# The third projection in lent score banks, value work of the first unit on GpSimd, and the choice of experts spread over the first steps

## The chip, the cores and the metric

One Trainium2 chip, one core of it. The time is that of the whole program on the device in microseconds, the median of several executions. TensorE (PE) multiplies, VectorE (DVE), ScalarE (ACT) and GpSimd (POOL) do the rest, each in the order of its own queue; semaphores tie them together. SyncE issues the DMAs.

## The reference, cut to what matters

Eight stages work one after the other on a residual of 2 sequences of 1024 tokens with 128 channels. The last and the last but two are the same stage with the same weights, and the change touches that one alone. It is attention with experts: 8 heads, 5 experts a head of which the best 3 count by a gate, 64 channels a head.

```python
ss = jax.nn.sigmoid(x @ Ws).reshape(b, t, H, E)
sd = jax.nn.sigmoid(x @ Wd).reshape(b, t, H, E)
ms, md = _topk_mask(ss, K), _topk_mask(sd, K)
q = jnp.einsum('bthed,bthe->bhtd', q5, sd * md)
k = jnp.einsum('bthed,bthe->bhtd', k5, ss * ms)
v = jnp.einsum('bthed,bthe->bhtd', v5, ss * ms)
attn = jax.nn.softmax(jnp.einsum('bhid,bhjd->bhij', q * scale, k), axis=-1)
out = jnp.einsum('bhij,bhjd->bihd', attn, v)
```

q5, k5 and v5 are the token times a weight of 5 x 64 columns for each head. The output of a head is sent through a second weight for each chosen expert and summed.

## The kernel before, in words

`expert_attention_stage` (from L2166) runs twice. A unit is a pair of heads of one sequence: 8 units of 8 tiles of 128 tokens, 64 tiles in all. A tile needs three projections (kinds 0 query, 1 key, 2 value), each for two heads: `project` (L2303) writes 320 columns into each of two PSUM banks, and DVE's `apply_gates` (L2607 for queries, L2610 for keys and values) multiplies both by the gates into `scratch`, the product; each kind has two buffers there. POOL's `sum_queries` (L2505 to L2507, three additions) and DVE's `sum_keys` (L2624) and `sum_values` (L2617) add the five experts.

Ahead of the steps the queries and keys of the first 8 tiles are made, then the 8 tiles of values, then queries and keys of 3 tiles more. Then 64 steps run, one a tile of queries. In step j PE makes the scores of j + 1 (L1504, two heads in banks 0 to 3), turns two blocks of the exponentials (L1515, bank 4), multiplies the values of step j - 1 (L1545, bank 5, 24 matmuls a head), and subtracts (L1524). Beside this it makes three projections, `beside(0)` to `beside(2)`: the value tile j + 8, the query and the key tile j + 11, each pair of heads in banks 6 and 7 (`spare`), each waiting until `product_ready` tells that the pair ahead is read. `first(j)` is the number of the step's first projection. From step 53 on only values are left, from 56 on nothing. In steps with t = j mod 8 of 2 and 6 `turn` (L2309) transposes four tiles of queries and of keys of the next unit, into banks 0 and 1, and ACT's `place` (L2430) copies them out.

DVE takes in step j: the maximum of the scores of head 0 (L1594), product, maximum of head 1, product, sum of values, reciprocal and routing of step j - 1 (`route`, L1601 and L1606), product, sum of keys. ACT takes: copy of the turned blocks (`act_copy`, L1571), exponential of head 0 (L1558), its high part in bf16 (`act_hi`, L1565), exponential of head 1, the rest (`act_rest`, L1575), high part of head 1. POOL takes: the low parts of step j (`pool_lo`, L1581, 768 and 1024 columns), counts, the sum of queries, and the sum of the routed output of j - 1 into z (L2493, from unit 2 on two sums, L2495 and L2496). SyncE sends high and low parts through the transposing DMA to PE's value matmuls.

At t = 0 and 4 half a unit's values are split in bf16: ACT makes the high half (`act_split_values`, L1619), POOL the low one (`pool_split_values`, L1623); for the first unit DVE does the latter (`dve_split_values`, L1628).

The choice of experts for a pair of heads: `compare` on DVE (four compares with `ahead` as output, L2587), 8 `count_duels` on POOL (L2516, L2518), `limit` on DVE (L2593), `keep` on POOL (L2525), and `chosen` lets DVE begin the queries of that pair.

Of the kernel before, what the change touches and what calls it, by code (L numbers as in the profile page):

```python
# [2165 lines left out]
def expert_attention_stage(core, tag):  # L2166
# [10 lines left out]
    with ExitStack() as ctx:  # L2177
# [29 lines left out]
        v_ready = sem("v_ready")  # L2207
# [24 lines left out]
        def last_of(tile, kind):  # L2232
# [5 lines left out]
            return 6 * T + 4 * (tile - T) + 2 * kind + 1 if tile < LEAD else first(tile - LEAD) + 2 * kind + 3  # L2238

# [34 lines left out]
        def _(pe):  # L2274
# [74 lines left out]
            for j in range(STEPS):  # L2349
                unit, t = j // T, j % T  # L2350
                turning = t in (2, 6) and unit + 1 < UNITS

                def beside(k):
                    n = first(j) + 2 * k
                    if n < first(j + 1):
                        pe.wait_ge(product_ready, n // 2)
                        for h in range(2):
                            project(n + h, spare[h])

                finishing = done_in(t) if unit + 1 == UNITS else ()  # L2360

                if j == STEPS - T:
                    pe.wait_ge(product_ready, first(STEPS) // 2)
                if j + 1 < STEPS:
                    if t in (3, 7) and unit + 1 < UNITS:
                        pe.wait_ge(qk_ready, (unit + 1) * 4 + t // 4 * 2 + 2)
                    hs.scores(pe, j + 1)
                beside(0)
# [7 lines left out]
                beside(1)  # L2376
                hs.subtract(pe, j)
                if turning:
                    pe.wait_ge(hs.exp_done, 2 * j + 3)
                    for i in range(2):  # L2380
                        turn(unit + 1, t // 4 * 2 + i, core.ps[i])
                if j:
                    hs.values(pe, j - 1, 1)
                beside(2)
# [13 lines left out]
        def _(act):  # L2398
# [48 lines left out]
            for i in range(2):  # L2447
                hs.act_split_values(act, 0, i, (v_ready, T // 2 * (i + 1)))
            for j in range(STEPS):
# [937 lines left out]
```

## Time and profile before

| | |
|---|---|
| median of 3 runs (lowest to highest) | 2641.14 us (2640.59 to 2646.53) |
| profiled execution: time, span | 2640.06 us, 2638.3 us |
| busy PE, PE weight load | 2353.3 us (89%), 1517.7 us (58%) |
| busy DVE, ACT, POOL | 2009.1 us (76%), 1480.1 us (56%), 1804.6 us (68%) |
| mean granted TensorE clock | 0.953 of full speed |
| L2303, projections of both stages | 508.7 us busy |
| L1581, low parts on POOL | 478.5 us busy |

The span is the time from the first instruction to the last on the core. Busy shares are over the whole span, so they average eight stages; what one step costs is read from the timelines of one step. In a timeline "x4" are four records of one group; a matmul in f32 leaves two records, so a projection of both heads is x4 and a set of scores x8. A tag in brackets gives the idle time before an instruction and what ended it.

### The profile page before, as it was taken

The page shows a single profiled execution, that of the slowest core. Times are in us where ns is not written, and L with a number is a line of the kernel's source. Part 1 is how long each engine was busy: PE and PEld are TensorE (multiplying, and loading weights), DVE is VectorE, ACT ScalarE, POOL GpSimd, SP SyncE. Part 2 cuts the span into 40 slices and gives each one's busy share as a digit, 9 for nine tenths or more (in the row PEclk, how much of TensorE's full clock was granted, in tenths as well). Part 3 has the DMA queues.
Part 4 walks back from the last instruction along what each step waited for, and adds up shares of the span by engine and source line. Part 5 has one row for each costly group of instructions (what it writes and reads, how often), then busy time and mean ns, then how long its engine had stood idle before and what let it go on. Part 6 is the DMA issues. An engine that isn't in the chain of part 4 may idle for free. (4 is left out here: it accounts for less than half of the span.)

```text
span 2638.3 us, 55375 instructions
## 1 busy us (share of the span) xinstructions
PE 2353.3 (89%) x21054; PEld 1517.7 (58%) x21054; DVE 2009.1 (76%) x3656; ACT 1480.1 (56%) x2085; POOL 1804.6 (68%) x1704
## 2 busy tenths in 40 slices
PE   6788777888799999999978999999879799999987
PEld 3555534644466667666655666666533556666655
DVE  7998555545677777777669999999567899999974
ACT  4222122332688888888834566556744256655665
POOL 0888300000699999999946899999820388999986
PEclk9899779889899999999989999999989899999999
DMA  1000000000698989889943666666710256666666
GB/s 46 1 1 0 1 24 14 1 24 17 134 160 151 163 148 162 159 151 163 145 112 64 113 113 117 119 116 113 140 40 0 70 95 117 113 119 116 117 113 122
DMA packets 829353, 243.48 MB, mean 92 GB/s; under 512 B 811528, under 2 KB 820232, under 8 KB 829088
## 3 DMA queue, kind: packets, MB, share of 16 engines
q1 hardware_dynamic: 829088, 239.93, 49.6%
q8 instruction: 168, 2.75, 0.4%
q14 instruction: 97, 0.79, 0.1%
HBM read 20.70 MB, written 1.05 MB: 8 GB/s over the span
## 5 line engine op out<-in xcount | busy, mean ns | idle before, releaser
L2303 PE MATMUL banks<-g_w,normed_t 128*128 128x320 f32 x1536 | 508.7, 457 | 23.9 <-DVE g_scratch L2610 11.0
L1581 POOL TENSOR_TENSOR g_p_lo<-g_p,g_p_hi 128x768 bf16<-128x768 f32 (+1 forms) x256 | 478.5, 1891 | 35.7 <-POOL g_z L2496 23.2
L1786 DVE TENSOR_REDUCE at_negmax<-banks 128x1 f32<-128x1024 f32 x256 | 301.4, 1219 | 154.6 <-PE banks L1698 154.6
L2303 PEld LDWEIGHTS banks<-g_w,normed_t 128*128 128x128 f32 x1536 | 262.3, 189 | 209.9 <-DVE g_scratch L2610 85.8
L1763 POOL TENSOR_TENSOR at_p_lo<-at_p,at_p_hi 128x640 bf16<-128x640 f32 x256 | 356.9, 1415 | 12.9 <-ACT at_p_hi L1751 11.3
L1594 DVE TENSOR_REDUCE g_negmax<-banks 128x1 f32<-128x1024 f32 x256 | 310.3, 1217 | 42.0 <-PE banks L1504 42.0
L1744 ACT ACTIVATE at_p<-banks,at_negmax 128x1024 f32<-128x1024 f32 x256 | 285.7, 1116 | 6.2 <-DVE at_negmax L1786 6.2
L1558 ACT ACTIVATE g_p<-banks,g_negmax 128x1024 f32<-128x1024 f32 x256 | 285.2, 1114 | 5.6 <-DVE g_negmax L1594 5.3
L1698 PE MATMUL banks<-at_k_t,at_q 64*128 64x512 f32 x1024 | 258.0, 622 | 18.2 <-POOL at_k_t L2047 9.5
L1504 PE MATMUL banks<-g_k_t,g_q 64*128 64x512 f32 x1024 | 254.4, 615 | 12.6 <-ACT g_p L1558 7.2
L1571 ACT CAST g_r_hi<-banks 128x256 bf16<-128x256 f32 x128 | 47.7, 372 | 380.8 <-PE banks L1515 380.8
L1565 ACT CAST g_p_hi<-g_p 128x768 bf16<-128x768 f32 (+1 forms) x256 | 241.7, 944 | 5.6 <-DMA g_t_lo<-g_p_lo 1.6
L1545 PE MATMUL banks<-g_v_hi,g_t_hi 128*128 128x65 bf16 x1792 | 191.5, 194 | 26.9 <-DMA g_t_lo<-g_p_lo 26.5
L2610 DVE TENSOR_TENSOR g_scratch<-banks,g_gate 128x640 f32<-128x640 f32 x256 | 209.7, 820 | 6.8 <-PE banks L2303 1.4
L1545 PEld LDWEIGHTS banks<-g_v_hi,g_t_hi 128*128 128x128 bf16 x1792 | 165.6, 98 | 51.4 <-DMA g_t_lo<-g_p_lo 37.1
L1545 PE MATMUL banks<-g_v_lo,g_t_hi 128*128 128x65 bf16 x1792 | 191.4, 194 | 0.0
L1770 POOL TENSOR_TENSOR at_u_lo<-at_u 128x768 bf16<-128x768 f32 x128 | 189.0, 1477 | 3.2 <-ACT at_u L1757 2.6
L1545 PE MATMUL banks<-g_v_hi,g_t_lo 128*128 128x65 bf16 x1792 | 190.3, 194 | 0.0
L1751 ACT CAST at_p_hi<-at_p 128x640 bf16<-128x640 f32 x256 | 185.9, 726 | 7.7
L1545 PEld LDWEIGHTS banks<-g_v_lo,g_t_hi 128*128 128x128 bf16 x1792 | 165.8, 98 | 2.4
L1545 PEld LDWEIGHTS banks<-g_v_hi,g_t_lo 128*128 128x128 bf16 x1792 | 166.0, 98 | 0.0
L1504 PEld LDWEIGHTS banks<-g_k_t,g_q 64*128 64x128 f32 x1024 | 88.3, 186 | 123.7 <-issue 96.2
(419 smaller groups left out, 5995.8 us busy)
## 6 DMA issues: line engine op xcount, KB each, us to landing
at_swapped<-at_crossed SPq DMA_DIRECT2D x128, 128.0 KB, 2.8
g_w<-in_ex_w SPq DMA_DIRECT2D x2, 2880.0 KB, 11.5
f_w<-in_W SPq DMA_DIRECT2D x2, 1024.0 KB, 5.5
at_rope<-in_rope SPq DMA_DIRECT2D x1, 2048.0 KB, 9.4
at_t_hi<-at_p_hi SPq DMA_TRANSPOSE x128, 3.7
at_t_lo<-at_p_lo SPq DMA_TRANSPOSE x128, 3.6
g_t_hi<-g_p_hi SPq DMA_TRANSPOSE x128, 4.3
g_t_lo<-g_p_lo SPq DMA_TRANSPOSE x128, 4.2
```

The lines of the kernel that those rows point to most:

```text
L1504: ins = self.nc.tensor.matmul(self.core.ps[2 * h + half], self.q[rows, b, t * P:(t + 1) * P], self.kt[rows, b, half * CHUNK:(half + 1) * C ...
L1545: ins = self.nc.tensor.matmul(self.sums[:, at:at + 65], p, v[:, b, k, h, :], start=(k == 0 and i == 0), stop=(k == self.T - 1 and i == 2))
L1558: self.nc.scalar.activation(self.p[:, j % 2, h, :], self.core.banks[:, 2 * h:2 * h + 2, :], ACT.Exp, bias=self.negmax[:, h:h + 1]).then_in ...
L1565: self.nc.scalar.copy(self.part(self.p_hi, j, h), self.p[:, j % 2, h, 0:self.WIDTH[h]]).then_inc(self.hi_ready, 1)
L1581: self.nc.gpsimd.tensor_tensor(self.part(self.p_lo, j, h), self.p[:, j % 2, h, 0:self.WIDTH[h]], self.part(self.p_hi, j, h), ALU.subtract) ...
L1594: self.nc.vector.tensor_reduce(self.negmax[:, h:h + 1], self.core.banks[:, 2 * h:2 * h + 2, :], AX.XY, ALU.max, negate=True).then_inc(self ...
L1698: ins = self.nc.tensor.matmul(self.core.ps[self.pair(j, h) + half], self.q[rows, b, t * P:(t + 1) * P], self.kt[rows, b, half * CHUNK:(hal ...
L1744: self.nc.scalar.activation(self.p[:, j % 2, h, :], self.core.banks[:, first:first + 2, :], ACT.Exp, bias=self.negmax[:, j % 2, h:h + 1]). ...
L1763: self.nc.gpsimd.tensor_tensor(self.p_lo[:, j % self.RING, h, :], self.p[:, j % 2, h, 0:self.BY_DMA * P], self.p_hi[:, j % self.RING, h, : ...
L1786: self.nc.vector.tensor_reduce(self.negmax[:, j % 2, h:h + 1], self.core.banks[:, first:first + 2, :], AX.XY, ALU.max, negate=True).then_i ...
L2303: nc.tensor.matmul(out[:, 0:ED], core.xt[:, at:at + P], w[:, kind * H + tile // (T * BATCH) * 2 + h, :], start=True, stop=True).then_inc(p ...
L2610: v.tensor_tensor((k_product if kind == 1 else v_product)[:, tile % 2], src.rearrange("p h (c e) -> p h c e", e=E), own.unsqueeze(2).to_br ...
```

## The change

- PE: in a step the first projection (values, still in banks 6 and 7) stands ahead of the scores, the second (queries, banks 6 and 7) behind them, the third (keys) goes to banks 0 and 1 and waits for head 0's exponential. The next scores wait for its product. `turn` uses banks 6 and 7 and waits for the second product. The subtraction stands at the end of the step, but in the last unit.
- DVE: product, sum of values, maximum, product, maximum, then the split of half the values at t = 0 and 4, routing, product, sum of keys. In steps 0 to 7 one compare (`duel`) follows for pairs 2 and 3; `limit` follows in steps 1, 13 and 22, not in 7 and 16.
- ACT: the copy of the turned blocks and `place` stand behind the exponential of head 0, the high half of the values behind the exponential of head 1.
- POOL: no splits in the steps; counts of pairs 2 and 3 in steps 5 to 12 and 14 to 21, `keep` in 3, 15 and 24.
- Ahead of the steps: POOL sums the values of tiles 1, 3, 5 and 7 (`sum_odd_values`) and splits the first unit; DVE compares pairs 0 and 1 alone; POOL counts pair 1 behind the queries of tile 9.

```diff
+
+        def own_sums(tiles):
+
+            return tiles - min(tiles, T) // 2
...
+                pairs = (first(j + 1) - first(j)) // 2
                 finishing = done_in(t) if unit + 1 == UNITS else ()
+
+                def both_heads(k, banks):
+                    for h in range(2):
+                        project(first(j) + 2 * k + h, banks[h])
                 if j == STEPS - T:
                     pe.wait_ge(product_ready, first(STEPS) // 2)
+                if t in (3, 7) and unit + 1 < UNITS:
+                    pe.wait_ge(qk_ready, (unit + 1) * 4 + t // 4 * 2 + 2)
+                if pairs:
+                    pe.wait_ge(product_ready, first(j) // 2 - (1 if j and first(j) - first(j - 1) == 6 else 0))
+                    both_heads(0, spare)
                 if j + 1 < STEPS:
-                    if t in (3, 7) and unit + 1 < UNITS:
-                        pe.wait_ge(qk_ready, (unit + 1) * 4 + t // 4 * 2 + 2)
+                    if pairs:
+                        pe.wait_ge(product_ready, first(j) // 2)
                     hs.scores(pe, j + 1)
-                beside(0)
+                if pairs == 3:
+                    pe.wait_ge(product_ready, first(j) // 2 + 1)
+                    both_heads(1, spare)
                 hs.transpose(pe, j)
...
                 if j:
                     hs.values(pe, j - 1, 0)
-                beside(1)
-                hs.subtract(pe, j)
                 if turning:
-                    pe.wait_ge(hs.exp_done, 2 * j + 3)
+                    pe.wait_ge(product_ready, first(j) // 2 + min(pairs, 2))
                     for i in range(2):
-                        turn(unit + 1, t // 4 * 2 + i, core.ps[i])
+                        turn(unit + 1, t // 4 * 2 + i, spare[i])
+                if unit + 1 == UNITS:
+                    hs.subtract(pe, j)
                 if j:
                     hs.values(pe, j - 1, 1)
-                beside(2)
+                if pairs == 3:
+                    pe.wait_ge(hs.exp_done, 2 * j + 3)
+                    both_heads(2, core.ps[0:2])
+                if unit + 1 < UNITS:
+                    hs.subtract(pe, j)
...
             for i in range(2):
-                hs.act_split_values(act, 0, i, (v_ready, T // 2 * (i + 1)))
+                act.wait_ge(v_odd, T // 4 * (i + 1))
+                hs.act_split_values(act, 0, i, (v_ready, own_sums(T // 2 * (i + 1))))
...
-                hs.act_copy(act, j)
+                if unit + 1 == UNITS:
+                    hs.act_copy(act, j)
                 for k, tile in finishing[0:1]:
                     place_out(k)
                 if not last:
                     hs.act_exp(act, j + 1, 0)
+                if unit + 1 < UNITS:
+                    hs.act_copy(act, j)
+                if t in (2, 6) and unit + 1 < UNITS:
+                    for i in range(2):
+                        place(unit + 1, t // 4 * 2 + i, core.ps[6 + i])
...
-                if t == 0 and unit:
-                    hs.act_split_values(act, unit, 1, (v_ready, (unit + 1) * T))
-                if t == 4 and unit + 1 < UNITS:
-                    hs.act_split_values(act, unit + 1, 0, (v_ready, (unit + 1) * T + T // 2))
                 if not last:
                     hs.act_exp(act, j + 1, 1)
+                if t == 0 and unit:
+                    hs.act_split_values(act, unit, 1, (v_ready, own_sums((unit + 1) * T)))
+                if t == 4 and unit + 1 < UNITS:
+                    hs.act_split_values(act, unit + 1, 0, (v_ready, own_sums((unit + 1) * T + T // 2)))
                 hs.act_rest(act, j)
-                if t in (2, 6) and unit + 1 < UNITS:
-                    for i in range(2):
-                        place(unit + 1, t // 4 * 2 + i, core.ps[i])
...
+            def sum_odd_values(tile):
+                pool.wait_ge(product_ready, (last_of(tile, 2) + 1) // 2)
+                part = v_product[:, tile % 2]
+                step(g.tensor_tensor(part[:, :, :, 0:2], part[:, :, :, 0:2], part[:, :, :, 2:4], ALU.add))
+                step(g.tensor_tensor(part[:, :, :, 0], part[:, :, :, 0], part[:, :, :, 1], ALU.add))
+                g.tensor_tensor(hs.v[:, tile, :, 0:D], part[:, :, :, 0], part[:, :, :, 4], ALU.add).then_inc(v_odd, 1)
+
...
-            for pair in range(2):
-                for k in range(8):
-                    count_duels(pair, k)
-            for pair in range(2):
-                keep(pair)
+            for k in range(8):
+                count_duels(0, k)
+            for tile in (1, 3):
+                sum_odd_values(tile)
+            keep(0)
+            for tile in (5, 7):
+                sum_odd_values(tile)
+            for i in range(2):
+                hs.pool_split_values(pool, 0, i)
             for tile in range(T, LEAD - 1):
                 sum_queries(tile)
+            for k in range(8):
+                count_duels(1, k)
...
-                if j % T == 0 and j:
-                    hs.pool_split_values(pool, j // T, 1)
-                if j % T == 4 and j // T + 1 < UNITS:
-                    hs.pool_split_values(pool, j // T + 1, 0)
-                if j < 18 and j % 9 < 8:
-                    count_duels(2 + j // 9, j % 9)
-                elif j < 18:
-                    keep(2 + j // 9)
+                if 5 <= j < 13:
+                    count_duels(2, j - 5)
+                elif 14 <= j < 22:
+                    count_duels(3, j - 14)
+                if j in (3, 15, 24):
+                    keep(1 + j // 12)
                 if j + LEAD - 1 < TOTAL:
                     sum_queries(j + LEAD - 1)
...
+                if kind == 2 and 2 <= tile < T + 2 and tile % 2:
+                    dve.wait_ge(v_odd, tile // 2)
+                elif kind == 2 and tile >= 2:
+                    dve.wait_ge(v_ready, own_sums(tile - 1))
+                elif tile >= 2:
+                    dve.wait_ge((q_ready, k_ready)[kind], tile - 1)
...
             def sum_values(tile):
+                if tile < T and tile % 2:
+                    return
...
             compare(0)
-            compare(1)
...
-            compare(2)
-            compare(3)
+            compare(1)
...
-                if tile in (4, 6):
-                    limit(tile // 2 - 2)
+                if tile == 4:
+                    limit(0)
...
-                else:
-                    for i in range(2):
-                        hs.dve_split_values(dve, 0, i)
...
-                        apply_gates(n, 6)
+                        apply_gates(n, 0 if k == 2 else 6)
                 finishing = done_in(t) if unit + 1 == UNITS else ()
+                beside(0)
+                if j + T < TOTAL:
+                    sum_values(j + T)
                 if j + 1 < STEPS:
                     hs.dve_max(dve, j + 1, 0)
-                beside(0)
+                beside(1)
                 if j + 1 < STEPS:
                     hs.dve_max(dve, j + 1, 1)
                 if unit + 1 == UNITS and t > 2:
                     add_out(*done_in(t - 1)[1])
-                beside(1)
-                if j + T < TOTAL:
-                    sum_values(j + T)
+                if t == 0 and unit:
+                    hs.dve_split_values(dve, unit, 1)
+                if t == 4 and unit + 1 < UNITS:
+                    hs.dve_split_values(dve, unit + 1, 0)
                 if j:
                     route(j - 1)
                 beside(2)
@@ -2701,8 +2736,12 @@
                     sum_keys(j + LEAD)
                 for k, tile in finishing[0:1]:
                     add_out(k, tile)
-                if j in (7, 16):
-                    limit(2 + j // 9)
+                if j < 2 * (E - 1):
+                    ins = duel(2 + j // (E - 1), j % (E - 1) + 1)
+                    if j % (E - 1) == E - 2:
+                        ins.then_inc(compared, 1)
+                if j in (1, 13, 22):
+                    limit(1 + j // 10)
```

## Rows read from the trace of the kernel before

**Rows 1.** Chain that ended last: start us, us, what; scores of four steps
```profile
2141.84 1.92 PE banks L1504 x8
...
2173.37 1.92 PE banks L1504 x8
...
2301.39 1.92 PE banks L1504 x8
...
2333.23 1.92 PE banks L1504 x8
```

**Rows 2.** Timeline of PE, one plain step: start us, us, engine, line, op, tiles, count
```profile
2206.03 1.99 PE L1504 MATMUL banks<-g_k_t,g_q 64*128 64x512 f32 x8
2207.94 1.34 PE L2303 MATMUL banks<-g_w,normed_t 128*128 128x320 f32 x4
2209.12 0.38 PE L1515 MATMUL banks<-identity,g_p 128*128 128x128 f32 x2
...
2210.20 1.34 PE L2303 MATMUL banks<-g_w,normed_t 128*128 128x320 f32 x4
...
2212.47 1.34 PE L2303 MATMUL banks<-g_w,normed_t 128*128 128x320 f32 x4
2213.74 1.56 PE L1504 MATMUL banks<-g_k_t,g_q 64*128 64x512 f32 x6
```

**Rows 3.** Timeline of DVE, the same step
```profile
2210.07 1.21 DVE L1594 TENSOR_REDUCE g_negmax<-banks 128x1 f32<-128x1024 f32 x1
2211.59 0.82 DVE L2607 TENSOR_TENSOR g_scratch<-banks,g_gate 128x640 f32<-128x640 f32 x1 [0.31 <-PE banks L2303]
2212.33 0.81 DVE L2617 TENSOR_REDUCE g_v<-g_scratch 128x128 f32<-128x640 f32 x1
2213.05 0.16 DVE L1601 RECIPROCAL g_recip<-banks 128x2 f32<-128x2 f32 x1
...
2214.17 0.81 DVE L2610 TENSOR_TENSOR g_scratch<-banks,g_gate 128x640 f32<-128x640 f32 x1
2215.02 0.82 DVE L2624 TENSOR_REDUCE g_tok<-g_scratch 128x128 f32<-128x640 f32 x1
2215.76 1.23 DVE L1594 TENSOR_REDUCE g_negmax<-banks 128x1 f32<-128x1024 f32 x1
```

**Rows 4.** Timeline of PE, a step that turns queries and keys
```profile
2203.17 1.04 PE L2309 MATMUL banks<-identity,g_tok 128*128 128x128 f32 x8
2204.05 0.19 PE L1545 MATMUL banks<-g_v_hi,g_t_hi 128*128 128x65 bf16 x1
...
2204.78 0.51 PE L2303 MATMUL banks<-g_w,normed_t 128*128 128x320 f32 x1
```

**Rows 5.** Timeline of POOL, a step of the fourth unit
```profile
2320.34 3.75 POOL L1581 TENSOR_TENSOR g_p_lo<-g_p,g_p_hi 128x768 bf16<-128x768 f32 x2 [0.24 <-POOL g_z L2496]
...
2327.84 3.75 POOL L1581 TENSOR_TENSOR g_p_lo<-g_p,g_p_hi 128x768 bf16<-128x768 f32 x2 [0.24 <-POOL g_z L2496]
```

**Rows 6.** Timeline of ACT, a step that splits half the values
```profile
2219.41 0.62 ACT L1619 CAST g_v_hi<-g_v 128x520 bf16<-128x520 f32 x1
2219.94 1.11 ACT L1558 ACTIVATE g_p<-banks,g_negmax 128x1024 f32<-128x1024 f32 x1
```

**Rows 7.** One line's instructions: L1628, the split on DVE (duration ns min/median/max)
```profile
L1628 DVE TENSOR_TENSOR g_v_lo<-g_v,g_v_hi x4: 686/954/1224, 1408.2 to 2111.2; 128x520 bf16<-128x520 f32 x4
```

**Rows 8.** Timeline of POOL beside the limit that ends the step with j = 7
```profile
2181.61 0.86 POOL L2493 TENSOR_TENSOR g_z<-g_routed 128x320 f32<-128x320 f32 x1 [0.83 <-DVE g_routed L1606]
2182.71 3.81 POOL L1581 TENSOR_TENSOR g_p_lo<-g_p,g_p_hi 128x768 bf16<-128x768 f32 x2 [0.24 <-POOL g_z L2493]
```

**Rows 9.** Timeline of DVE, the same moment
```profile
2183.03 1.51 DVE L2593 TENSOR_SCALAR g_mask<-g_mask 128x320 f32<-128x320 f32 x1
```

**Rows 10.** Timeline of DVE, first unit ahead of the steps
```profile
2091.17 3.62 DVE L2587 TENSOR_TENSOR g_ahead<-g_gate 128x256 bf16<-128x256 f32 x8
...
2110.60 1.83 DVE L1628 TENSOR_TENSOR g_v_lo<-g_v,g_v_hi 128x520 bf16<-128x520 f32 x2
```

More of the change, by code:

```diff
@@ L2206, in expert_attention_stage @@
         q_ready, k_ready = sem("q_ready"), sem("k_ready")
-        v_ready = sem("v_ready")
+        v_ready, v_odd = sem("v_ready"), sem("v_odd")
         qk_full, qk_ready = sem("qk_full"), sem("qk_ready")
@@ L2351, in _ @@
                 turning = t in (2, 6) and unit + 1 < UNITS
[L2353 to L2358, printed above, removed]
+                pairs = (first(j + 1) - first(j)) // 2
                 finishing = done_in(t) if unit + 1 == UNITS else ()
+                def both_heads(k, banks):
+                    for h in range(2):
+                        project(first(j) + 2 * k + h, banks[h])
                 if j == STEPS - T:
                     pe.wait_ge(product_ready, first(STEPS) // 2)
+                if t in (3, 7) and unit + 1 < UNITS:
[3 more added lines that the diff above has]
+                    both_heads(0, spare)
                 if j + 1 < STEPS:
-                    if t in (3, 7) and unit + 1 < UNITS:
-                        pe.wait_ge(qk_ready, (unit + 1) * 4 + t // 4 * 2 + 2)
+                    if pairs:
+                        pe.wait_ge(product_ready, first(j) // 2)
                     hs.scores(pe, j + 1)
-                beside(0)
+                if pairs == 3:
+                    pe.wait_ge(product_ready, first(j) // 2 + 1)
+                    both_heads(1, spare)
                 hs.transpose(pe, j)
@@ L2583, in compare, with duel @@
             def compare(pair):
+                for d in range(1, E):
+                    ins = duel(pair, d)
+                ins.then_inc(compared, 1)
+            def duel(pair, d):
                 own, beat = gate[:, pair, :, rows_left(pair)], ahead[:, pair, :, rows_left(pair)]
-                for d in range(1, E):
-                    ins = v.tensor_tensor(beat[:, :, :, duels(d)], own[:, :, :, 0:E - d], own[:, :, :, d:E], ALU.is_ge)
-                ins.then_inc(compared, 1)
+                return v.tensor_tensor(beat[:, :, :, duels(d)], own[:, :, :, 0:E - d], own[:, :, :, d:E], ALU.is_ge)
             def limit(pair):
@@ L2600, in apply_gates @@
                     dve.wait_ge(chosen, (1, 2, 4, 6).index(tile // T) + 1)
-                if tile >= 2:
-                    dve.wait_ge((q_ready, k_ready, v_ready)[kind], tile - 1)
+                if kind == 2 and 2 <= tile < T + 2 and tile % 2:
[4 more added lines that the diff above has]
+                    dve.wait_ge((q_ready, k_ready)[kind], tile - 1)
                 row = 2 * row_of(tile)
@@ L2703, in _ @@
                     add_out(k, tile)
-                if j in (7, 16):
-                    limit(2 + j // 9)
+                if j < 2 * (E - 1):
+                    ins = duel(2 + j // (E - 1), j % (E - 1) + 1)
+                    if j % (E - 1) == E - 2:
+                        ins.then_inc(compared, 1)
+                if j in (1, 13, 22):
+                    limit(1 + j // 10)
             add_out(*done_in(T - 1)[1])
```

## Prediction, made before the changed kernel was run

> **What bounds the kernel now.** I read the busy shares first: TensorE (PE) is busiest, VectorE (DVE) and GpSimd (POOL) follow, none is full. So I went to the chain that ended last and, in it, to the starts of the scores, one set a step. Four steps take 31.53 us in the first unit and 31.84 in the fourth [rows 1]. Three of the four are plain steps of 7.71 (scores at 2206.03 and 2213.74 [rows 2]); the rest of a group is 8.4 to 8.7 in the step that turns queries and keys.
>
> Then the timelines of PE and DVE for one plain step, side by side, to see who waits. 7.71 is a closed loop. From one scores to the next PE runs: scores 1.91, first projection until its product can start on DVE (about 1.38, as the third shows), product 0.82 plus a hop of 0.06, second projection 1.39 (2210.20 to the product at 2211.59), product 0.88 (to 2212.47), third projection 1.27 (to 2213.74). 1.91 + 1.38 + 0.88 + 1.39 + 0.88 + 1.27 = 7.71 [rows 2, 3]. All three projections go through the same two banks, so each waits for the product that empties them. Neither engine is full inside: this ping-pong sets the pace.
>
> **The change, plain step.** The third projection goes to banks 0 and 1 once head 0's exponential is out, the first moves ahead of the scores. The loop above is cut. What is next? DVE, added from start to start of neighbours that don't wait: product to its own sum 0.85 (2214.17 to 2215.02), sum to maximum 0.74, maximum about 1.13 (1.21 busy, next one starts 0.08 before its end), product 0.74 (2211.59 to 2212.33), maximum 1.13, reciprocal and routing 1.12 (2213.05 to 2214.17), product and its sum 0.85, sum 0.74 [rows 3]: 7.30. (The order of before would be 0.12 less: its value sum doesn't follow its own product directly.) PE: scores 1.91, three projections of 1.18 (2207.94 to 2209.12), two sets of values of 0.73 (2204.05 to 2204.78), transposes and subtraction some 0.33, an estimate under their busy times: 7.24 [rows 2, 4]. So DVE bounds at 7.30, PE has 0.06 to spare, and the new loop (scores 2.02 from 2213.74 to 2215.76, maximum 1.21, exponential 1.11, projection 1.38, product 0.88, and hops [rows 2, 3, 6]) is 6.7 and not the bound. Gain 0.40 in each of 53 steps: -21 us a stage. Bounds: 0.26 (a PE restart costs up to 0.09 a time) to 0.47 (PE alone), -14 to -25.
>
> **Turning.** 0.88 of PE (2203.17 to 2204.05 [rows 4]); before it cost 0.61 (31.53 less four times 7.71, the rest was slack). Now PE has 0.06, so nearly all shows: 0.94, with the wait for the second product. +0.33 x 14 = +4.6; bounds 0 to +7.
>
> **POOL.** In units with two sums per route POOL repeats after 7.50 (2320.34 to 2327.84 [rows 5]), four times is 30.0, with a split of half the values on top, against a group of 31.84. I put the 0.31 by which this group is longer than one of the first unit [rows 1] down to it. The split leaves POOL, ten groups in units 2 to 6: -3.5 with some rounding up for the longer ones (bounds 0, -4). POOL's 30.0 a group is covered by the longer groups below. The later POOL counts (j = 14 to 21) lie in that cover too; without it they would cost their 3 us.
>
> **The splits on DVE, the largest term.** The split now stands on DVE between the second maximum and the routing, and waits for the high half. ScalarE (ACT) makes that half after head 1's exponential, and this exponential needs the very maximum that stands before the split on DVE. So DVE, in order, waits out a round trip: maximum 1.21, exponential 1.11, cast 0.62 [rows 3, 6], two or three hops and the tail of the cast of head 0 before it, 3.1 to 3.2 from the maximum's start, where the routing would have started after 1.13. That is 2.0 idle, and the split itself 0.69 [rows 7]: 2.7. Behind it on DVE are queued the routing, the third product, the key sum; PE's next scores wait for that product, so nothing hides it, DVE being the bound. Before, the same work sat on POOL, and DVE never waited. 14 a stage, the last of them in a step without projections at 1.5: 13 x 2.7 + 1.5 = +36.6. Bounds: 2.4 (every hop free, PE's slack taken off) to 3.2 (a GpSimd instruction to wait for as well), +32 to +44. The trace of before has no such wait; this is built from its durations and the order in the code.
>
> **Duels and limits.** Eight duels (pairs 2 and 3) leave the stretch ahead of the steps, where eight took 3.62 [rows 10], 0.44 each, and go one to a step at DVE's end in steps 0 to 7. What lies there is shown by the limit at the end of step 7: it started at 2183.03, 0.32 after POOL had begun its low parts, right after the route's sum [rows 8],, and took 1.51 [rows 9], because it waited for that first low part. The duel stands 0.3 behind the same point; DVE's order up to it is unchanged. I take 1.5 each and 10.5 for eight, since POOL is late in the first two steps. Bounds: 0.35 (no wait, a little under the 0.44) to 2.3 (the longer low part, over half of 3.81, and the duel), +3 to +18. The limits are three in the steps and not two, all after the same point: 2.2 (the first comes right behind a duel and meets the longer low part) + 1.5 + 1.5, against 1.4 for the two before, of which only the one shown found POOL at a low part: +3.8 (0 to +5).
> The Trainium skill (SBUF — State Buffer, Who interferes with whom) says that a Vector instruction with two SBUF inputs contends with a GpSimd one that reads SBUF, and that whoever starts first holds the shared pair for the whole instruction. By that rule a duel waits for a low part to end; with the 0.44 of a duel among short counts the same eight would cost 3.5. The trace agrees with the rule: two splits of one shape on DVE took 0.69 and 1.22 [rows 7].
>
> **Ahead of the steps.** DVE loses four compares up front (1.1, an estimate under 4 x 0.44, since POOL is idle there), two splits (1.83 [rows 10]) and four value sums (0.72 each to the next, as 2212.33 to 2213.05 [rows 3]); the two compares at 3.62 become one, which gains nothing, since the first scores come no earlier. An odd tile's sum on POOL is three additions, 512 elements in all: by the 0.86 for 320 elements [rows 8] about 1.4, with hops 1.7, where DVE's took 0.81, and the product two tiles later waits for it. 1.1 + 1.8 + 2.9 less about 1.3 of such waits is 4.5. But POOL now counts pair 1 (5 us) after that and only then makes the first low parts: their transpose lands late for the second step, 1 us back. -3.5; bounds 0 and -5.8.
>
> **Sum.** A stage: -21 + 4.6 - 3.5 + 36.6 + 10.5 + 3.8 - 3.5 = +27.5. Two stages of the same code: +55. The profiled execution has 2640.06 us (span 2638.3), within 0.05% of the median 2641.14, so 2640 + 55 = 2695.
>
> **Rivals.**
> Faster: the waits fall where DVE would idle anyway. A split then costs its 0.61 to the next instruction, a duel or a limit 0.35. Per stage -21 + 4.6 - 3.5 + 8.5 + 2.8 - 0.3 - 4.5 = -13.4, two stages 2613. For it: in a plain step of before DVE idles, 0.31 ahead of a product alone [rows 3]. Against: that idle belongs to the loop that is cut. It decides if the plain step comes out near 7.7 by DVE idling ahead of the routing. 0.15.
> Even: the split costs half, 1.3 to 1.4, because half of its wait hides in PE's values and third projection, and the duels cost little: 36.6 becomes 19, 10.5 becomes 3, the limits 0: -1.4 a stage, 2637. 0.10.
> Slower but less: the split waits, the duels and limits don't meet POOL (0.35 each): 10.5 becomes 2.8, 3.8 becomes about 0.3: +16.3 a stage, 2673. For it: the order of the steps moves POOL's low parts against DVE's end. Against: both follow the routing, as before. 0.17.
> The change doesn't do what it says: lending banks 0 and 1 puts the third product in front of the next scores, and through maximum, exponential and projection this closes a loop of 6.7 which, with the transposes and values that PE does in order inside it, is the old 7.71. No gain in the plain step: +27.5 + 21 a stage, 2737. 0.05.
> Forecast as summed: 0.53; its own range 2660 to 2718, the outer bounds not all at once.
>
> **Chances and range.** A measurement tells 0.3%, 8 us, from no change. Slower by more: 0.53 + 0.17 + 0.05 = 0.75. Within: 0.08 of the even case. Faster: 0.15 + 0.02. The range 2636 to 2722 takes in the forecast, the lesser slowdown and the even case and leaves out the fast one and the last, 2 in 10.
>
> **What would show it.** Plain steps of 7.3 from scores to scores, with DVE without gaps. Twice in eight steps a gap of about 2 us on DVE ahead of L1628, released by ACT's cast of the values, and scores 2.7 apart more than plain. In steps 0 to 7 compares of 1.3 to 1.7 on DVE that end just after a low part on POOL. First scores of step 0 some 4 us earlier after the stage's start. Wrong would be: DVE's split starts right behind the maximum; plain steps at 7.7; or compares of 0.45.

## The result and the profile after

The changed kernel takes 2719.09 us (median of 4 runs, 2713.78 to 2721.32) against 2643.30 us for the kernel before (median of 4 runs beside it, 2640.59 to 2646.53): ratio 1.0283, 95% interval 1.0262 to 1.0304. It is slower by 76 us. The profiled execution has a span of 2718.2 us, 79.9 more than before. Beside the first experiments two of 19 executions of the kernel before took 3384 and 7869 us, in a slow state; no comparison below uses them.

The page of the changed kernel: busy shares, granted clock in 40 slices, and the chain that ended last by engine.

```profile
span 2718.2 us, 55504 instructions
PE 2360.6 (87%) x21054; PEld 1519.9 (56%) x21054; DVE 2035.1 (75%) x3672; ACT 1469.0 (54%) x2085; POOL 1790.0 (66%) x1704
PEclk9998778888899999999999999999989999999998
DVE 10%; PE 5%; issue 4%; ACT 1%; POOL 1%; DMA 1%; DVEq 0%; ACTq 0%; POOLq 0%
```

Before, the chain was PE 8%, POOL 7%, DVE 3%. PE, the busiest engine, is busy for 7 us more in a span that is 80 longer, so it stands idle for 73 us more. DVE now leads the chain.

The starts of the scores give the place. In the second stage four steps in a row are 8.43 to 8.47 (a turning step), 7.21 (plain), 9.86 (with a split) and 8.7 to 8.9 (the step behind the split): 34.2 to 34.4, where the kernel before had 31.84 [rows 1]. Here are rows of TensorE, VectorE and ScalarE from a step with a split (scores to scores 9.86) and the one behind it (8.86) (columns: start and duration in us, engine, line, operation, tiles; in brackets the idle time before it and what ended it).

```profile
2404.33 1.99 PE L1504 MATMUL banks<-g_k_t,g_q 64*128 64x512 f32 x8
2409.10 1.32 PE L2307 MATMUL banks<-g_w,normed_t 128*128 128x320 f32 x4
2410.36 1.24 PE L2307 MATMUL banks<-g_w,normed_t 128*128 128x320 f32 x4
2414.19 3.57 PE L1504 MATMUL banks<-g_k_t,g_q 64*128 64x512 f32 x8 [2.58 <-DVE g_scratch L2644]
2423.05 1.99 PE L1504 MATMUL banks<-g_k_t,g_q 64*128 64x512 f32 x8
```

```profile
2408.52 1.22 DVE L1594 TENSOR_REDUCE g_negmax<-banks 128x1 f32<-128x1024 f32 x1
2411.58 0.70 DVE L1628 TENSOR_TENSOR g_v_lo<-g_v,g_v_hi 128x520 bf16<-128x520 f32 x1 [1.84 <-ACT g_v_hi L1619]
2412.39 1.01 DVE L1606 SCALAR_TENSOR_TENSOR g_routed<-banks,g_recip,g_mask 128x320 f32<-128x320 f32 x2
2413.32 0.81 DVE L2644 TENSOR_TENSOR g_scratch<-banks,g_gate 128x640 f32<-128x640 f32 x1
```

```profile
2409.91 1.13 ACT L1558 ACTIVATE g_p<-banks,g_negmax 128x1024 f32<-128x1024 f32 x1
2410.91 0.63 ACT L1619 CAST g_v_hi<-g_v 128x520 bf16<-128x520 f32 x1
```

Read the second fence first. VectorE's second maximum ends at 2409.74. Its next instruction is the split at 2411.58, and the gap of 1.84 ends with ScalarE's cast, which stands behind the exponential at 2409.91, which in turn waited for that maximum. This is the round trip of the prediction: a result of VectorE goes to ScalarE, and VectorE waits for what ScalarE makes behind it. Behind the split come the routing and the third product (2413.32 to 2414.13), and TensorE, which finished its projection at 2411.60, waits 2.58 for it. Over the whole kernel:

```profile
L1628 DVE TENSOR_TENSOR g_v_lo<-g_v,g_v_hi x28: 699/701/916, 1462.0 to 2648.5; 128x520 bf16<-128x520 f32 x28
  ACT g_v_hi L1619: 52.7, 28
```

These are 28 splits, and VectorE stood idle for 52.7 us before them.

Now the scores at 2414.19 take 3.57 us where their neighbours take 1.99, with the same eight records and the same shapes. The view by windows shows why (columns: window, length, busy time and count of PE, PEld, DVE, ACT, POOL, then the granted clock as a share of full speed, DMA share, GB/s).

```profile
2385.00:2414.00 29.00, 26.43 (x273) 17.32 (x269) 25.88 (x37) 18.82 (x27) 24.62 (x26) 1.00 0.58 112
2414.00:2418.00 4.00, 3.81 (x9) 1.31 (x10) 2.72 (x5) 0.00 (x0) 3.68 (x4) 0.57 0.60 114
2418.00:2423.00 5.00, 5.00 (x63) 3.67 (x62) 4.78 (x7) 3.96 (x6) 3.54 (x5) 1.00 0.48 92
```

The granted clock is 1.00, then 0.57 over the 4 us in which the scores run (most of that time at the lower level, 1.2 GHz, for 2.4), then 1.00 again. These are the 1.4 to 1.7 us by which the step behind the split is longer than a plain one, and it is the item that the prediction did not have. In the steps of both stages 21 sets of scores are slow in this way, by 31 us together.

The duel of step 1 of the second stage and the limit behind it, and then GpSimd's low parts beside them:

```profile
2173.65 0.82 DVE L2660 TENSOR_REDUCE g_tok<-g_scratch 128x128 f32<-128x640 f32 x1
2174.39 1.57 DVE L2618 TENSOR_TENSOR g_ahead<-g_gate 128x192 bf16<-128x192 f32 x1
2175.81 2.20 DVE L2623 TENSOR_SCALAR g_mask<-g_mask 128x320 f32<-128x320 f32 x1
2177.93 0.81 DVE L2644 TENSOR_TENSOR g_scratch<-banks,g_gate 128x640 f32<-128x640 f32 x1
```

```profile
2173.98 3.84 POOL L1581 TENSOR_TENSOR g_p_lo<-g_p,g_p_hi 128x768 bf16<-128x768 f32 x2 [0.24 <-POOL g_z L2509]
```

The duel takes 1.57 and the limit behind it 2.20 (2175.81 to 2178.01); the pair of low parts runs from 2173.98 to 2177.82 (3.84), and the limit ends 0.19 behind it. Where nothing meets it a limit takes 0.32. [rows 8, 9] showed the same meeting for one limit of before.

### The profile page after: what moved, and what is told of

The parts are those of the page before. It is cut to its first block and busy times, and to the rows that moved or that the text cites. A ratio compares the mean times of both kernels' runs of the same rounds, so it can differ in the third digit from the quotient of the medians.

```text
span 2718.2 us, 55504 instructions
## 1 busy us (share of the span) xinstructions
PE 2360.6 (87%) x21054; PEld 1519.9 (56%) x21054; DVE 2035.1 (75%) x3672; ACT 1469.0 (54%) x2085; POOL 1790.0 (66%) x1704
## 5 line engine op out<-in xcount | busy, mean ns | idle before, releaser
L2307 PE MATMUL banks<-g_w,normed_t 128*128 128x320 f32 x1536 | 492.2, 451 | 30.5 <-DVE g_scratch L2644 24.7
L1504 PE MATMUL banks<-g_k_t,g_q 64*128 64x512 f32 x1024 | 285.7, 682 | 79.5 <-DVE g_scratch L2644 67.6
L1504 PEld LDWEIGHTS banks<-g_k_t,g_q 64*128 64x128 f32 x1024 | 98.5, 206 | 205.5 <-DVE g_scratch L2644 116.9
L2511 POOL TENSOR_TENSOR g_z<-g_z,g_routed 128x320 f32<-128x320 f32 x96 | 82.8, 862 | 104.6 <-DVE g_routed L1606 104.5
```

The costliest lines, as they stand in the source:

```text
L1504: ins = self.nc.tensor.matmul(self.core.ps[2 * h + half], self.q[rows, b, t * P:(t + 1) * P], self.kt[rows, b, half * CHUNK:(half + 1) * C ...
L2307: nc.tensor.matmul(out[:, 0:ED], core.xt[:, at:at + P], w[:, kind * H + tile // (T * BATCH) * 2 + h, :], start=True, stop=True).then_inc(p ...
```

## The experiments

Times below are medians beside runs of the kernel before on the same chip. Its median was 2645.0, 2643.0, 2643.8 and 2639.2 in the four groups of runs, so kernels of different groups are compared by their ratio to it; 0.001 is 2.6 us. The theory: VectorE's split waits out a round trip over ScalarE; TensorE stands still behind it and comes back at the lower clock; and duels and limits wait for low parts.

### e1: nobody waits for the cast

```
 ScalarE, step j:
+    act_split_values(...)     # ahead of exp(j + 1, 0)
     act_exp(j + 1, 0)
     ...
     act_exp(j + 1, 1)
-    act_split_values(...)
     act_rest(j)
```

> The changed kernel with one move: ScalarE makes the high half of the values ahead of the first exponential of the step, where it stands idle (3.11 us ahead of the exponential at 2407.91 in the changed kernel) and where all sums it needs are a step old. VectorE's split stays where it is. Theory 1 (the split waits out the round trip, TensorE is idle behind it and comes back at a lower granted clock): the idle ahead of L1628 (1.88 each) falls to about 0, the split step costs 0.6 over a plain one and not 2.65, the step behind it nothing and not 1.5; 3.5 in each of 13 places and two stages, 92 us, less some that GpSimd gives back: 2625 to 2645. Theory 2 (the split hurts by its own 0.7 on a full VectorE, and the slow scores come from elsewhere): at most the idle of 1.9 is saved and the slow scores stay, 2719 less 53: 2666 or more.

Measured: 2639.17 us, ratio 0.9985 (0.9970 to 0.9999). One moved cast gives back 79 us (1.0283 less 0.9985), more than the whole slowdown. The lines of one split step, VectorE, ScalarE's cast and TensorE's scores:

```profile
2362.98 1.21 DVE L1594 TENSOR_REDUCE g_negmax<-banks 128x1 f32<-128x1024 f32 x1
2364.11 1.04 DVE L1628 TENSOR_TENSOR g_v_lo<-g_v,g_v_hi 128x520 bf16<-128x520 f32 x1
2359.13 0.65 ACT L1619 CAST g_v_hi<-g_v 128x520 bf16<-128x520 f32 x1
2367.07 1.99 PE L1504 MATMUL banks<-g_k_t,g_q 64*128 64x512 f32 x8 [1.00 <-DVE g_scratch L2644]
2374.35 1.99 PE L1504 MATMUL banks<-g_k_t,g_q 64*128 64x512 f32 x8
```

The cast ended 4 us before it is needed and the split starts right behind the maximum. TensorE waits 1.00 and not 2.58, and its scores take 1.99. The split step is 8.28 and the one behind it 7.28. The split still costs 0.6 to 1.0 (steps of mostly 7.92 to 8.29, where e2, below, has 7.31): at 1.04 it is longer than the 0.70 it takes after a wait; GpSimd had begun a short sum (0.73 long) 0.24 before it. Theory 2, at least 2666, is out.

### e2: the split back on GpSimd

This is e1 and, besides:

```
 GpSimd, step j, behind both low parts:
+    pool_split_values(...)
 VectorE, between second maximum and routing:
-    dve_split_values(...)
```

> As e1_cast_early, and the 14 splits of a stage go from VectorE back to GpSimd, behind its low parts, where the kernel before had them. Theory 1 (GpSimd had little room: 7.5 a step in the fourth unit, and my -3.5 a stage for what leaves it): VectorE gains 0.6 a split, but GpSimd's group of four steps becomes 30.0 + 0.9 to 1.2 against VectorE's 30.0: within 5 us of e1_cast_early, 2625 to 2645. Theory 2 (GpSimd has room to spare, VectorE is the only bound): 14 x 2 x 0.6 less than e1_cast_early, 17 us.

Measured: 2648.52 us, ratio 1.0014 (1.0000 to 1.0029), 8 us more than e1, outside the 5 that theory 1 allowed and on the other side of what theory 2 said. The split step is now 7.31, but of the last nine turning steps of the second stage, nearly all 8.48 in e1, six are 8.6 to 9.7 and one is 12.04. That one, on TensorE:

```profile
2341.81 0.38 PE L1515 MATMUL banks<-identity,g_p 128*128 128x128 f32 x2
2344.32 0.20 PE L1545 MATMUL banks<-g_v_hi,g_t_hi 128*128 128x65 bf16 x1 [2.13 <-DMA g_t_lo<-g_p_lo]
2345.05 1.46 PE L2313 MATMUL banks<-identity,g_tok 128*128 128x128 f32 x8
```

TensorE waits 2.13 for the DMA of a low part: GpSimd works without a pause there and delivers late, and in the chain that ended last GpSimd has 11% of the span (3% in e1) and VectorE 4% (11% in e1). So moving the splits off GpSimd was worth something once VectorE did not wait for them.

### e3 and e8: duels ahead of the steps, and duels in another place of the step

```
 e3, VectorE ahead of the steps:       e8, VectorE in step j:
     compare(1)                        +    duel(...)        # steps 0 to 7
+    compare(2)                             route(j - 1)
+    compare(3)                             beside(2); sum_keys(...)
 in step j:                            -    duel(...)
-    duel(...)
```

> The changed kernel with the compares of pairs 2 and 3 back ahead of the steps, in one piece, as before; none in the steps. Theory 1 (a duel at the end of VectorE's step waits for a low part on GpSimd, 1.6 each in the trace where its own work is 0.45): steps 0 to 7 lose 1.15 to 1.5 each, 8 x 1.3 = 10.5 a stage, against 3.6 ahead of them: -7 a stage, or -14: 2705. Theory 2 (the waits lie where VectorE idles anyway): steps the same, 3.6 a stage more: 2726.

> The changed kernel with the duel of steps 0 to 13 moved on VectorE from the end of the step to just ahead of the routing, behind the second maximum, where GpSimd is past its low parts (in the trace they end 0.3 ahead of the second maximum's end). Same operations, no other change. Theory 1 (a duel is long because it meets a low part): duels of steps 2 to 7 take 0.45 to 0.6 and not 1.6, each saves about 1.1, 7 of them in two stages: 2719 less 15 = 2704. Theory 2 (a duel in the steps costs its 1.6 wherever it stands): 2719.

Measured: e3 2703.87 us, ratio 1.0209 (1.0182 to 1.0236); e8 2703.82 us, ratio 1.0223 (1.0201 to 1.0245). Both gain 15 us by the medians (20 and 16 by the ratios). The duels stand in steps 0 to 7, four of each pair; the 13 in the text for e8 is a slip, and the 7 counts the long ones of a stage. In e3 the stretch from the first scores to the second is 26.54 and not 23.98, so the steps themselves gave back about 10 a stage (steps 1 to 9 of the second stage 76.1 and not 86.6). e8 keeps every operation and moves a duel behind the second maximum; this is its row for the eight duels of the second stage:

```profile
L2618 DVE TENSOR_TENSOR g_ahead<-g_gate x8: 419/468/647, 2154.9 to 2214.5; 128x256 bf16<-128x256 f32 x2, 128x192 bf16<-128x192 f32 x2, 128x128 bf16<-128x128 f32 x2, 128x64 bf16<-128x64 f32 x2
```

and the same row of the changed kernel:

```profile
L2618 DVE TENSOR_TENSOR g_ahead<-g_gate x8: 565/1605/1659, 2166.1 to 2234.5; 128x256 bf16<-128x256 f32 x2, 128x192 bf16<-128x192 f32 x2, 128x128 bf16<-128x128 f32 x2, 128x64 bf16<-128x64 f32 x2
```

(least, median and greatest duration in ns). The same operation takes 468 ns where it doesn't meet a low part and 1605 where it does: a duel's price is its place. The first stage has an exception that says the same: e8's duel of step 0 starts at 1419.51, 0.26 behind the start of a low part of 2.13, and takes 2.15.

### e4: TensorE kept busy in the stall

```
 TensorE, step j behind a split, ahead of the scores:
+    pe.wait_ge(exp_done, 2 * j + 2)
+    for i in range(44):
+        matmul(core.ps[3][:, 384:512], minus, minus, start=True, stop=True)
     pe.wait_ge(product_ready, first(j) // 2)
     scores(pe, j + 1)
```

> The changed kernel with work added: in each step whose scores wait for the late third product, TensorE makes 44 matmuls of 128 columns whose result nobody reads, in the 2.58 us in which it was idle. Theory 1 (the granted clock falls because TensorE stood still before): the scores behind the filler take 1.9 to 2.0 and not 3.57, the record of the granted clock stays full there, VectorE's waits of 1.9 stay: 24 to 28 places by 1.5, -30 to -40: 2680 to 2690. Theory 2 (the scores are slow for another reason, the late operands or the transfers beside them): scores still at 3.5, and the time the same or more, 2719 to 2730.

Measured: 2689.50 us, ratio 1.0165 (1.0148 to 1.0182), 30 us faster with 1056 matmuls more. TensorE in one such place, and the windows around it:

```profile
2325.16 2.62 PE L2373 MATMUL banks<-g_minus 128*128 128x128 bf16 x44
2327.96 1.99 PE L1504 MATMUL banks<-g_k_t,g_q 64*128 64x512 f32 x8 [0.18 <-DVE g_scratch L2648]
2335.24 1.99 PE L1504 MATMUL banks<-g_k_t,g_q 64*128 64x512 f32 x8
```

```profile
2325.00:2328.00 3.00, 2.82 (x48) 2.49 (x45) 2.64 (x6) 1.48 (x3) 1.99 (x3) 1.00 0.91 176
2328.00:2331.00 3.00, 3.00 (x12) 1.46 (x13) 2.97 (x4) 0.00 (x0) 2.68 (x4) 1.00 0.95 135
```

Scores start as late as in the changed kernel (the split step is 9.86 in both), the granted clock stays at 1.00 (over the whole execution it is 0.951, in the changed kernel 0.94, before 0.953), they take 1.99, and the step behind is 7.28 and not 8.7 to 8.9. So the slow scores come from TensorE's standing still before them (though not every such stop is followed by slow scores, see the last section), and of the 79 us of e1 some 30 are clock and some 50 are VectorE's wait.

### e5 and e7: both causes out, and the lent banks taken back

e5 is e1 and e3 together. e7 is e5 with

```
-    pe.wait_ge(exp_done, 2 * j + 3)
-    both_heads(2, core.ps[0:2])
+    pe.wait_ge(product_ready, first(j) // 2 + 2)
+    both_heads(2, spare)              # in a turning step also behind the copies of the turn
```

> e1_cast_early and e3_duels_early together: the cast ahead of the first exponential, the compares of pairs 2 and 3 ahead of the steps; VectorE's splits stay in the steps. Theory 1 (two separate causes): the 15 us of e3_duels_early come off e1_cast_early's 2639: 2624. Theory 2 (with VectorE's waits gone GpSimd is the bound of the first steps, where its low parts and counts lie, and the compares hide under it): 2635 to 2640.

> e5_both with the third projection back in the two spare banks, with the waits for the product that empties them; all else as in e5_both, with the first projection ahead of the scores. Theory 1 (the lent banks make the plain step 7.2 and not 7.7): +0.4 to 0.5 in some 53 steps and two stages, +42 to +53 over e5_both. Theory 2 (the new order alone, first projection ahead of the scores, brings it): within 5 us of e5_both.

Measured: e5 2621.26 us, ratio 0.9912 (0.9885 to 0.9939); the two causes add. e7 2740.37 us, ratio 1.0360 (1.0333 to 1.0388), 118 us more than e5: over twice what theory 1 said. A plain step is 8.43, longer than the 7.71 of before. Here are TensorE and VectorE there:

```profile
2359.87 1.34 PE L2307 MATMUL banks<-g_w,normed_t 128*128 128x320 f32 x4 [0.96 <-DVE g_scratch L2646]
2361.14 1.99 PE L1504 MATMUL banks<-g_k_t,g_q 64*128 64x512 f32 x8
```

```profile
2361.25 0.82 DVE L2646 TENSOR_TENSOR g_scratch<-banks,g_gate 128x640 f32<-128x640 f32 x1 [0.51 <-PE banks L2307]
2363.16 1.22 DVE L1594 TENSOR_REDUCE g_negmax<-banks 128x1 f32<-128x1024 f32 x1 [0.23 <-PE banks L1504]
```

The first projection, now ahead of the scores, waits 0.96 for the third product, and the scores are queued behind it; then VectorE waits for both. The new order is worse than the old without the lent banks (8.43 against 7.71) and better with them (7.21 to 7.28). So the lending is worth 1.2 a step in the new order. The order of before with lent banks was not run, so that the new order is needed for the gain is not shown.

### e6: the splits on VectorE in the kernel before

This is the kernel before with the splits on VectorE between value sum and routing and the cast ahead of the first exponential, and nothing else.

> The kernel before with one part of the change: the 14 splits of a stage on VectorE between the value sum and the routing and not on GpSimd; ScalarE's high half is made ahead of the first exponential, so that nobody waits for it. Banks, order of TensorE and compares as before. Theory 1 (the splits cost by the wait, not by their work; VectorE idles 0.3 a plain step in the order of before, GpSimd gains the 0.31 a group that I gave it): 28 places at 0.4 to 0.7 less 20 groups at 0.31, +5 to +13: 2650. Theory 2 (in this order GpSimd's release is worth nothing and the split meets a low part of 1.6 to 2.1): 28 x 1.3: 2680.

Measured: 2646.19 us, ratio 1.0010 (0.9998 to 1.0021), 3 us more than the kernel before, a little under the 5 to 13 of theory 1 and far from theory 2. A split step is 8.17 (+0.46), and a turning step in the fourth unit 8.32 where it was 8.71: what GpSimd's release gives (0.39 a group; I had 0.31) nearly pays for the split. The split itself starts right behind the value sum and takes 0.69, with nobody to wait for. One step grows more, in both stages: that behind the limit of step 16, from 7.82 to 11.06. The limit took 0.35 before; now GpSimd has begun a low part 0.31 ahead of it, and it takes 1.51. The split, and this limit:

```profile
2319.95 0.69 DVE L1628 TENSOR_TENSOR g_v_lo<-g_v,g_v_hi 128x520 bf16<-128x520 f32 x1
2256.63 1.51 DVE L2589 TENSOR_SCALAR g_mask<-g_mask 128x320 f32<-128x320 f32 x1
```

### e9 to e12: better than both

e9 is e5 with each unit's first split moved on VectorE from t = 4 to the turning step t = 6. e10 is e9 with the turn behind the second set of values and ScalarE's copies of it behind the second exponential. e11 is e10 with the limits ahead of the routing, e12 is e9 with the same.

> e5_both with the split of each unit's first half of the values (7 a stage) moved on VectorE from the step t = 4 to t = 6, in which TensorE turns keys and VectorE idles 0.79 ahead of its reciprocal. Theory 1 (the split costs what it adds to a full VectorE, and here there is room): the step of the split falls from 7.9 to 8.3 to 7.2 to 7.3, the turning step grows by 0.3 at most: 14 places at 0.7 to 0.9, -10 to -13: 2610. Theory 2 (the split at t = 6 meets a low part or delays the routing as much as it did): within 3 us of e5_both, 2621.

> e9_split_turning with the turn of two tiles behind the second set of values on TensorE, and ScalarE's copies of it behind head 1's exponential. In the trace the turn waited 0.29 for the second product. Theory 1 (that wait is on the path): 28 turning steps at 0.2 to 0.3, -6 to -8 from e9_split_turning. Theory 2 (TensorE's 0.29 only changes where VectorE waits, and the copies now hold up the next first projection): 0 to +8.

> e10_turn_late with the three limits of a stage moved from the end of VectorE's step, where they start beside GpSimd's first low part, to just ahead of the routing. Theory 1 (as with the duels, the 2.2 and 1.5 us are waits for a low part): 2.2 + 1.5 + 1.5 becomes three times 0.4 to 0.5, less than 1 us of it given back: -3 a stage, -5 to -7. Theory 2 (they wait for GpSimd's counts or cost the same there): 0.

> e9_split_turning with the three limits ahead of the routing, and the turn of keys where the changed kernel has it: the parts that each gained, together. Theory 1 (the gains add): 2616 less the 3 us that the limits gave in e11_limits: 2613, a ratio of 0.989 to the kernel before. Theory 2 (without the late turn the limits find no room, or the compares of a low part only move elsewhere): 2616 to 2620.

Measured: e9 2615.82 us, ratio 0.9899 (0.9868 to 0.9929), 5 us below e5 by the medians, half of what was expected, and by the intervals not certain; the steps that the splits left are 7.3 and the turning steps mostly stay at 8.5, but the steps with the second halves' splits are still 7.8 to 8.5. e10 2626.99, ratio 0.9940 (0.9918 to 0.9961), a loss of 11: the sign and the cause of theory 2, and more than its 8. Its turning step is 9.06:

```profile
2323.63 1.34 PE L2307 MATMUL banks<-g_w,normed_t 128*128 128x320 f32 x4 [0.76 <-ACT g_k_t L2442]
```

The late turn's copies on ScalarE hold up the next first projection, which needs the same banks, by 0.76. e11 2623.73, ratio 0.9923 (0.9894 to 0.9953), 3 us below e10, between the two theories and by the intervals not certain; the limits fall from a median of 1178 to 495 ns. e12, the best: 2611.57 us, ratio 0.9898 (0.9882 to 0.9915), 1.0% faster than the kernel before and nearly 4% than the changed one. Its median is 4 below e9's, but the ratios are the same, so that these 4 are the limits' is not shown.

## Why the prediction was right, and where its steps were not

The forecast was 2695, slower by 55; measured is 2719, slower by 76. The sign and the mechanism of most of it (the round trip, the duels) held. The size came in by little: 2719 is 3 us inside the upper end of the range, 2722, and 1 above the 2718 that the forecast as summed gave itself. Of the 21 us missing, the clock alone (some 30) is more than all.

- **Plain step, 7.30.** Measured 7.21 to 7.28. VectorE has no gap of more than 0.04 there, as forecast, but TensorE has none either: the 7.21 is TensorE's own work, which the sum had at 7.24, while VectorE took 7.37 from one value product to the next, 0.16 more, beside it. That VectorE alone bounds the step, as the sum said, the trace does not show. That the loop is cut by the lent banks is shown by e7, but the price without them was not 7.71: the order was changed too, and alone it costs 0.7. The rival "lent banks close a loop of 7.71" was wrong in the changed kernel. These are the two value products of VectorE around the plain step whose scores start at 2431.48:

```profile
2431.99 0.81 DVE L2644 TENSOR_TENSOR g_scratch<-banks,g_gate 128x640 f32<-128x640 f32 x1
2439.36 0.81 DVE L2644 TENSOR_TENSOR g_scratch<-banks,g_gate 128x640 f32<-128x640 f32 x1
```

- **Turning, +0.94.** Measured +1.2 (8.43 to 8.48 against 7.21 to 7.28). The turn starts 0.05 behind the end of the second product and 0.32 behind the start of the last of the first values, which follow one another every 0.03; for that wait of 0.29 the sum had only 0.06. The term was mis-sized by some 0.3 x 28 = 8 us. What a turn cost before was misread too: 31.53 less four times 7.71 is 0.69 and not 0.61, though 0.61 is what three of the first five turning steps of that stage show (8.32). e10 shows that the wait can't simply be moved past. TensorE and VectorE in the turning step:

```profile
2427.06 0.19 PE L1545 MATMUL banks<-g_v_hi,g_r_lo 128*128 128x65 bf16 x1
2427.38 1.09 PE L2313 MATMUL banks<-identity,g_tok 128*128 128x128 f32 x8
2426.51 0.82 DVE L2641 TENSOR_TENSOR g_scratch<-banks,g_gate 128x640 f32<-128x640 f32 x1
```

- **Splits, +2.7.** Measured +2.65, idle 1.88 (forecast 2.0), work 0.70 (0.69). e1 shows that most of it is the wait: without it a split costs 0.6 to 1.0. The last split of a stage, charged at 1.5, lengthened its step by only 0.4 (6.73 against 6.32 in e5).
- **The step behind the split, +0.** This is the step that failed. The sum took TensorE's durations from rows at full clock and let it stand idle for 2 us at no price. In steps 9 to 53 of the second stage 8 of 11 groups have this step at 8.6 to 8.9 and three at 7.3; in the first stage it is 9 of 11. No rival of the prediction had it either. e4 removes it alone: a group there is 9.86 + 7.28 + 8.48 + 7.21 = 32.83. The prediction's own group, four times 7.30 and 0.94 and 2.7, is 32.84 (its two errors in the plain and the turning step cancel, which is luck), and e4's 2689.5 us is 5.5 from the forecast.
- **POOL, -3.5.** e6 shows 0.39 a group where I had 0.31, and e2 what it costs when the splits go back. That is in the old order and in another kernel; in the changed kernel itself the term can't be read by itself.
- **Duels, 1.5 each, and limits.** Measured 1.55 to 1.66 for seven of eight and 0.57 for the first, 11.8 for the eight (forecast 10.5); 2.20, 1.43 and 0.53 for the three limits (forecast 2.2, 1.5, 1.5). e8 shows the mechanism: moved past the low parts a duel is 0.47. By the Trainium skill (SBUF — State Buffer, Who interferes with whom) a VectorE instruction with two SBUF inputs contends with a GpSimd one that reads SBUF, and the ports that they share are an exclusive lock; the pair of numbers 0.47 and 1.6 agrees. That one holds them for its whole instruction, which the prediction took from the page, is said there of another mode; e8's duel that takes 2.15 beside a low part of 2.13 shows it here. The limit, which reads one tile only, is held as well (0.32 and 2.20). The rival "don't meet" was wrong.
- **Ahead of the steps, -3.5.** The first scores come 1.5 earlier after the stage's start and the second 1.3 more (23.98 against 25.32), together 2.8. The 4 us that I named as a sign did not appear as such. The sum said that compares at this place gain nothing when they become fewer, but they stand ahead of the first maximum, and the second interval goes with their number: 23.98 with four, 25.32 with eight (the kernel before), 26.54 with twelve (e3), 0.3 a compare. That gain is in none of the terms, and the 1 us that I charged to the later POOL count is not seen; so the total of 3.5 is near 2.8 partly by luck.
- **The rivals.** "Faster" assumed that the waits fall in time in which VectorE is idle. They did not; that its time, 2613, is near what e9 and e12 reach when the waits are taken out (2616 and 2612) is chance, since these move operations as well.

## What to carry to other kernels

Before an operation is moved to another engine, look at what its input waits for there: if that input is made behind a step that needs this engine's own last result, the engine waits out a round trip; make the input a step early, in the other engine's idle time. When a sum puts a stall on the matmul engine, price what comes behind it at the lower clock too. And where two engines hold each other off, a short instruction's cost is its place: shift it past the long one before you shift it to another part of the program.

## What the runs showed of the hardware that I had not expected

TensorE's granted clock fell after an idle of only 2.58 us in an otherwise busy stretch, and stayed down for most of the scores behind it, which cost 1.4 to 1.7 us. It did not do so each time. These three are all scores behind a step with a split, the first behind one at t = 4, the others behind one at t = 0, after the same idle:

```profile
2278.03 3.61 PE L1504 MATMUL banks<-g_k_t,g_q 64*128 64x512 f32 x8 [2.58 <-DVE g_scratch L2644]
2313.69 1.99 PE L1504 MATMUL banks<-g_k_t,g_q 64*128 64x512 f32 x8 [2.57 <-DVE g_scratch L2644]
2448.55 3.68 PE L1504 MATMUL banks<-g_k_t,g_q 64*128 64x512 f32 x8 [2.58 <-DVE g_scratch L2644]
```

with these granted clocks for the first two, 0.58 and 1.00:

```profile
2278.00:2282.00 4.00, 3.98 (x10) 1.54 (x11) 2.71 (x4) 0.00 (x0) 3.76 (x3) 0.58 0.57 109
2313.00:2317.00 4.00, 3.31 (x14) 1.71 (x15) 3.93 (x5) 0.00 (x0) 3.76 (x3) 1.00 0.60 115
```

Neither the length of the idle nor the place in the step decides between them; what does was not followed up. In e1, whose idles ahead of the scores behind a split are 0.6 to 1.2, and in e7, with idles up to 1.83, no single matmul of the scores takes over 693 ns in some 45 to 50 steps of the second stage, so none ran at the lower clock. These are the rows (least, median and greatest duration of one matmul in ns, then the first and the last start in us):

```profile
L1504 PE MATMUL banks<-g_k_t,g_q x398: 589/589/693, 2140.8 to 2539.7; 64*128 64x512 f32 x199
```

```profile
L1504 PE MATMUL banks<-g_k_t,g_q x360: 589/589/693, 2200.8 to 2595.4; 64*128 64x512 f32 x180
```

A shorter idle is no safety, though: in the last steps of e5's first stage the scores at 1849.00, behind an idle of 1.55, took 3.51, and behind the same idle of 1.55 in its second stage 1.99. In e2 the idle of 2.13 ahead of the values was followed by a lower clock (0.76 in 2344 to 2347), and the turn at 2345.05 took 1.46 where it takes 1.09. In e4 filling the idle with 44 small matmuls of no use was worth 30 us.
